# A layer with a top-2 mixture of experts on one core: slot tokens through an inverse table, outputs added to the residual in DRAM

## The chip, the core and the metric

The kernel runs on one core of a Trainium2 chip. Its engines are TensorE (PE), VectorE (DVE), ScalarE (ACT), GpSimd (POOL) and SyncE (SP); each runs its own instruction stream and waits on semaphores. The metric is the device time in microseconds (us) of one execution. Before the change: median 1988.87 us of 3 runs (1988.52 to 1989.82).

## The reference

Input x is 2 x 1024 tokens of 256 floats. First comes a linear-attention layer, then a transformer layer with softmax attention and a mixture of experts, each inside `x + layernorm(layer(layernorm(x)))`. The change is in the experts' part and in what follows it:

```
def moe(h, gate_w, w1, w2, w3):          # E, F, TOPK = 8, 1024, 2
    t = h.reshape(-1, hd)
    probs = softmax(t @ gate_w)
    topw, topi = top_k(probs, TOPK)
    topw = topw / sum(topw)
    combine = zeros((T, E)).at[arange(T)[:, None], topi].add(topw)
    up = einsum('th,ehf->etf', t, w1)
    gated = relu(up) * einsum('th,ehf->etf', t, w3)
    down = einsum('etf,efh->eth', gated, w2)
    return einsum('eth,te->th', down, combine)
h = x + attention(rmsnorm(x, ln1_w), wq, wk, wv, wo)
ffn = h + moe(rmsnorm(h, ln2_w), gate_w, w1, w2, w3)
out = x + layernorm(ffn)                 # x: the input of this block, before its own layernorm
```

## The kernel before

The order of work is written out by hand, one stream for each engine, with semaphores between them. In time it has four stages.

1. Linear attention, up to about 245 us. At its end POOL issues one DMA that writes zeros over all of `xs`, a DRAM buffer of 39 x 128 rows of 1 KB (line 423). While it runs, SP loads the output weights of the second attention, `wo2` (line 326).
2. Softmax attention, 128 tiles, up to about 1432 us. PE is the busiest engine. The residual stream h stands in SBUF as `acc`, 16 tiles of 128 tokens x 256.
3. Router. PE turns h and multiplies it with the gate; DVE works out the two best experts of each token, their shares `topw`, and for each of the 4096 token-expert pairs the row it has in a list sorted by expert, `rowi` (lines 887 to 941). The list is cut into NS = 39 slots of 128 rows; each slot has one expert, `slotei`, and 39 is enough for any routing. Rows of a slot that no token takes are padding. ACT scales h to `t_all` (line 633). Then POOL issues 32 indirect DMAs (line 465), each of which scatters 128 rows of `t_all` to their rows of `xs`. 128 rows of 1 KB are one DMA.
4. Experts, slot by slot. Three chains u = 0, 1, 2 take 13 slots each in turn, so that work item e is slot e // 3 + (e % 3) x 13. SP loads the slot's expert (w1, w3 and w2, 1 MB each, only where the expert changes in the chain), waits for all 32 scatters (line 346) and loads the slot's 128 rows of `xs` (line 347). PE turns them (line 1281), multiplies with w1 and w3 (line 1297), and after relu (ACT, line 652) and product (DVE, line 950) with w2 (line 1306). ACT copies the result to `y_sb` (line 656) and POOL stores it to `ys`, also in DRAM (line 471). When all slots are stored, POOL gathers for each of 16 token tiles two blocks of 128 rows from `ys` (line 477, 32 indirect DMAs), and DVE, a quarter of the tiles at a time, adds them with their weights to `acc` (line 958), takes mean and variance (963, 967), normalises (973), adds to `x_all` (976), and SP stores the tile (line 354).

Every engine stream is in order, so an instruction that waits holds all those behind it.

## Time and profile before

| | us |
|---|---|
| median of 3 runs | 1988.87 |
| the profiled execution, its own time | 1999.07 |
| its span (first to last instruction) | 1997.4 |
| PE busy in the span | 1812.1 (91%) |
| DVE busy | 1061.8 (53%) |
| ACT busy | 910.8 (46%) |
| POOL busy | 234.5 (12%) |
| mean DMA rate over the span | 34 GB/s |

The profile is of one execution, recorded by the hardware profiler; it ran some 10 us longer than the median of the runs without one. Busy shares are means over the four stages. The page's picture of 40 slices of about 50 us shows PE busy at nine tenths or more in nearly all of them, with two places where it isn't: slice 30 (from about 1448 us), where PE is idle and its granted clock is 0.5, and the last one and a half slices, where only DVE and POOL work.

### The profile page before, as it was taken

Reading aid. Unit: us, or ns where it says so; the run is one execution under the profiler, and the core shown is the slowest. Engines: PE = TensorE matmul, PEld = TensorE weight load, DVE = VectorE, ACT = ScalarE, POOL = GpSimd, SP = SyncE. Lnnn points to the kernel's source line nnn. Section 1 sums busy time; section 2 is a strip of 40 time slices with the busy share of each in tenths; the row PEclk is TensorE's granted clock in tenths of the full one; section 3 lists DMA queues with packets and bytes.
Section 4 is the critical chain, followed back from the end, with each engine's and each line's share of the span. In section 5 each row is a group of like instructions: output and inputs, shape, how many; then the busy total and the mean of one; then the engine's idle time right before and its main releaser. Section 6 shows DMA issues by size and latency. Waiting matters only on the chain.

```text
span 1997.4 us, 32462 instructions
## 1 busy us (share of the span) xinstructions
PE 1812.1 (91%) x12222; PEld 1425.7 (71%) x12222; DVE 1061.8 (53%) x2489; ACT 910.8 (46%) x2028; POOL 234.5 (12%) x368
## 2 busy tenths in 40 slices
PE   6999689999999999999999999999907999999970
PEld 5666467777777777777777777777807999999960
DVE  3666566766766766676676676676420111111106
ACT  3433265665666665665565566565511112211210
POOL 2222210000000000000000000000051000000014
PEclk9999899999999999999999999999958999999985
DMA  2000030000000000000000000000034042022413
GB/s 80 0 0 0 28 118 1 9 1 9 1 1 9 1 1 9 1 1 9 1 1 9 1 1 1 1 1 1 1 134 161 24 152 84 26 89 75 161 32 110
DMA packets 44296, 67.22 MB, mean 34 GB/s; under 512 B 9952, under 2 KB 34528, under 8 KB 44192
## 3 DMA queue, kind: packets, MB, share of 16 engines
q1 hardware_dynamic: 35920, 45.11, 6.9%
q0 software_dynamic: 6208, 18.62, 2.8%
q10 hardware_dynamic: 2064, 2.10, 0.3%
q8 instruction: 66, 1.08, 0.2%
q14 instruction: 38, 0.31, 0.1%
HBM read 140.52 MB, written 16.52 MB: 79 GB/s over the span
## 4 chain that ended last, share of the span: by engine, by line
PE 82%; DVE 6%; issue 3%; POOL 3%; ACT 2%; DMA 1%; SPq 1%; another core or an unknown queue 0%; DVEq 0%; POOLq 0%; ACTq 0%
PE wide L1297 14%; PE bank L1219 13%; PE bank L1207 11%; PE bank L1159 8%; PE wide L1191 8%; PE bank L1306 7%; PE wide L1192 7%; PE bank L1228 6%; PE wide L1026 2%; PE bank L1015 2%; POOL xs L465 1%; PE bank L1204 1%; POOL arena L477 1%; ACT qhl L583 1%; PE bank L1083 1%
## 5 line engine op out<-in xcount | busy, mean ns | idle before, releaser
L823 DVE CUSTOM_DVE_ANT_0 arena<-wide,arena 128x896 f32<-128x896 f32 (+7 forms) x512 | 383.6, 754 | 225.1 <-PE wide L1192 221.1
L589 ACT ACTIVATE arena<-arena,nmax 128x896 f32<-128x896 f32 (+7 forms) x512 | 397.1, 776 | 177.4 <-DVE nmax L823 174.3
L1191 PE MATMUL wide<-khi,qhl 128*128 128x512 f32 (+3 forms) x768 | 346.2, 452 | 1.7 <-DVE qhl L816 1.7
L1207 PE MATMUL bank<-ident,arena 128*128 128x128 f32 x2304 | 308.4, 273 | 0.0
L597 ACT COPY arena<-bank 128x512 f32<-128x512 f32 (+1 forms) x352 | 191.7, 545 | 215.4 <-PE bank L1207 206.2
L1297 PEld LDWEIGHTS wide<-wo,arena 128*128 128x128 f32 x2496 | 287.0, 193 | 3.2 <-issue 1.3
L1297 PE MATMUL wide<-wo,arena 128*128 128x128 f32 x2496 | 287.3, 276 | 0.9 <-ACT wo L641 0.9
L1219 PE MATMUL bank<-arena,vt 128*64 128x256 f32 x2304 | 276.9, 385 | 0.0
L950 DVE TENSOR_TENSOR wo<-wide,wo 128x512 f32<-128x512 f32 x78 | 54.0, 692 | 415.3 <-PE wide L1297 415.3
L1207 PEld LDWEIGHTS bank<-ident,arena 128*128 128x128 f32 x2304 | 262.2, 140 | 16.8 <-issue 0.4
L1192 PE MATMUL wide<-klo,qhl 128*128 128x512 f32 (+3 forms) x768 | 256.1, 347 | 0.0
L831 DVE COPY arena<-bank 128x512 f32<-128x512 f32 (+1 forms) x352 | 222.8, 638 | 9.2 <-PE bank L1207 8.5
L1219 PEld LDWEIGHTS bank<-arena,vt 128*64 128x64 f32 x2304 | 154.2, 136 | 91.0 <-issue 20.1
L1191 PEld LDWEIGHTS wide<-khi,qhl 128*128 128x128 f32 x768 | 145.1, 189 | 89.7 <-issue 65.9
L1192 PEld LDWEIGHTS wide<-klo,qhl 128*128 128x128 f32 x768 | 145.8, 190 | 37.1 <-issue 22.5
L1228 PE MATMUL bank<-wo,oT 128*128 128x256 f32 x512 | 135.1, 386 | 12.5 <-DVE oT L848 10.6
L455 POOL COPY arena<-rinv 128x256 f32<-128x256 f32 x128 | 50.9, 398 | 787.2 <-DVE rinv L844 785.2
L1306 PE MATMUL bank<-arena,wo 128*128 128x256 f32 x624 | 141.2, 379 | 0.0
L1306 PEld LDWEIGHTS bank<-arena,wo 128*128 128x128 f32 x624 | 115.5, 190 | 14.1
L652 ACT ACTIVATE wo<-wide 128x512 f32<-128x512 f32 x78 | 46.6, 597 | 173.3 <-PE wide L1297 173.3
L1159 PE MATMUL bank<-rT_all,wq_g 128*128 128x512 f32 x256 | 123.7, 607 | 0.3
L1228 PEld LDWEIGHTS bank<-wo,oT 128*128 128x128 f32 x512 | 87.1, 190 | 25.5 <-DVE oT L848 15.0
(192 smaller groups left out, 1708.4 us busy)
## 6 DMA issues: line engine op xcount, KB each, us to landing
arena<-in_L_ffn_w SPq DMA_DIRECT2D x117, 1024.0 KB
wo<-xs SPq DMA_DIRECT2D x40, 128.0 KB, 2.0
xs<-zeros POOLq DMA_DIRECT2D x1, 4992.0 KB, 20.7
ys<-y_sb POOLq DMA_DIRECT2D x39, 128.0 KB, 2.0
x_all<-in_L_attn_x ACTq DMA_DIRECT2D x1, 2048.0 KB, 9.7
wq_g<-in_L_ffn_wq SPq DMA_DIRECT2D x8, 256.0 KB, 3.3
wo<-in_L_ffn_wo SPq DMA_DIRECT2D x16, 128.0 KB, 8.1
out<-x_all SPq DMA_DIRECT2D x16, 128.0 KB
```

Source lines behind the costliest of these rows:

```text
L589: nc.scalar.activation(probs[t % 2][:, h, 0:w], probs[t % 2][:, h, 0:w], ACT.Exp, bias=nmax[:, t % 2, h:h + 1], scale=-1.0, accum_out=rsum ...
L597: nc.scalar.copy(*turned_to(t, m)).then_inc(S("pT_even"), 1)
L823: nc.vector.tensor_tensor_reduce(out=probs[t % 2][:, h, 0:w], in0=score_bank(t, h)[:, 0:w], in1=causal[:, SEQ - w:SEQ], scale=-1.0, scalar ...
L831: nc.vector.tensor_copy(*turned_to(t, m)).then_inc(S("pT_odd"), 1)
L1159: ins = mm(to, w, rT_all[:, k, at:at + HALF], start=(k == 0), stop=(k == KB - 1))
L1191: mm(dst, q, khi[:, lo:lo + cols], start=True, stop=False)
L1192: ins = mm(dst, q, klo[:, lo:lo + cols], start=False, stop=True)
L1207: ins = nc.tensor.transpose(to[:, h * P:(h + 1) * P], probs[t % 2][:, h, m * P:(m + 1) * P], ident[:])
L1219: ins = mm(bank[2][u * DH:(u + 1) * DH, 0:2 * P], vt[:, n % 2, m], pT[t % 2][m][:, u * 2 * P:(u + 1) * 2 * P], start=(m == 0), stop=(m == ct))
L1228: ins = mm(bank[2][:, 2 * P:2 * P + D], oT[:, j], wo2[:, t // (BATCH * TB), j], start=(j == 0), stop=(j == 1))
L1297: ins = mm(wide[:, at + half, f * P:(f + 1) * P], w[:, k, (half * 4 + f) * P:(half * 4 + f + 1) * P], sT[u][:, k], start=(k == 0), stop=(k ...
L1306: ins = mm(bank[u][:, 0:D], gated[:, f], w2_e[u][:, f], start=(f == 0), stop=(f == FB - 1))
```

## The change

Both scatters of data through DRAM go; three things come in their place.

- The table `rowi` (token to row) is inverted into a table with a column for each slot and a partition for each place in it, which says which token stands there. This is done on PE: with a one-hot matrix of a pair's place in its slot (`inplace`, bf16) as weights and a one-hot matrix of its slot, multiplied with tile number or token number (`worth`, bf16), as the moving side, 32 accumulated matmuls give the token of each row of each slot (`found`, line 1373 of the new kernel), and 32 more the weight of each (`wfound`, line 1377), the float32 weight being split into three bf16 parts. DVE makes the one-hot matrices and reads the results. `fromrow` is the table that is read from (padding reads token 0), `torow` the one that is added to (padding goes to 128 spare rows).
- `t_all` is stored to DRAM (`tbuf`) as it is, in four DMAs of 512 KB. POOL gathers the 128 rows of a slot with one indirect DMA, three slots ahead. `acc` is stored to DRAM too (`hbuf`), in two DMAs of 1 MB.
- ACT scales a slot's output with the weights of its rows as it takes it from PSUM, and POOL adds the 128 rows to their rows of `hbuf` with one indirect DMA that accumulates, each issued only when the one before has landed (semaphore `added`). At the end SP loads `hbuf` back to `acc` in four DMAs, and the final layernorm goes in pairs of tiles: statistics on DVE, normalising on ACT, the last add on POOL. ACT's and POOL's slot loops are written out instead of looping.

The diff, cut to its core:

```
+        tbuf = nc.dram_tensor("tbuf", (NT * P, D), F32, kind="Internal").ap()
+        hbuf = nc.dram_tensor("hbuf", (NT * P + P, D), F32, kind="Internal").ap()
...
 # SP
+            sp.wait_ge(S("acc_done"), BATCH * NKV * TB - TB)
+            sp.dma_start(h_v[:, 0:TB], acc[:, 0:TB]).then_inc(S("h_stored"), 16)
+            sp.wait_ge(S("acc_done"), BATCH * NKV * TB)
+            sp.dma_start(h_v[:, TB:NT], acc[:, TB:NT]).then_inc(S("h_stored"), 16)
+            for i in range(4):
+                tiles = slice(i * (NT // 4), (i + 1) * (NT // 4))
+                sp.wait_ge(S("t_ready"), i + 1)
+                sp.dma_start(t_v[:, tiles], t_all[:, tiles]).then_inc(S("t_stored"), 16)
             sp.wait_ge(S("slots_known"), 1)
...
-                    sp.wait_ge(S("xs_scattered"), 16 * TOPK * NT)
-                    sp.dma_start(xs_sb[u], xs_v[:, bass.ds(slot, 1)].rearrange("p o d -> p (o d)")).then_inc(S(f"xs_loaded{u}"), 16)
...
+            sp.wait_ge(S("added"), 16 * NS)
+            for q in range(4):
+                tiles = slice(q * (NT // 4), (q + 1) * (NT // 4))
+                sp.dma_start(acc[:, tiles], h_v[:, tiles]).then_inc(S(f"h_loaded{q}"), 16)
...
 # POOL
-            gp.dma_start(xs.rearrange("(s p) d -> p s d", p=P), zeros[:]...).then_inc(S("xs_zeroed"), 16)
...
+            def gather(e):
+                u, slot = e % UR, (e // UR + e % UR * RUN) % NS
+                nc.gpsimd.indirect_dma_start(out=xs_sb[u], out_offset=None, in_=tbuf,
+                                             in_offset=bass.IndirectOffsetOnAxis(ap=fromrow[:, slot:slot + 1], axis=0)).then_inc(S(f"xs_loaded{u}"), 16)
+            gp.wait_ge(S("t_stored"), 16 * 4)
+            gp.wait_ge(S("fromrow_ready"), 1)
+            for e in range(UR):
+                gather(e)
+            gp.wait_ge(S("torow_ready"), 1)
+            gp.wait_ge(S("h_stored"), 32)
+            for e in range(NS):
+                u, slot = e % UR, e // UR + e % UR * RUN
+                if e + UR <= NS:
+                    gp.wait_ge(S("sT_psum"), e + 1)
+                    gather(e + UR)
+                gp.wait_ge(S(f"y_ready{u}"), e // UR + 1)
+                if e:
+                    gp.wait_ge(S("added"), 16 * e)
+                nc.gpsimd.indirect_dma_start(out=hbuf, out_offset=bass.IndirectOffsetOnAxis(ap=torow[:, slot:slot + 1], axis=0),
+                                             in_=y_sb[u][:], in_offset=None, compute_op=ALU.add).then_inc(S("added"), 16)
+            for q in range(NT // 2):
+                gp.wait_ge(S("fn_ready"), q + 1)
+                nc.gpsimd.tensor_tensor(x_all[:, 2 * q:2 * q + 2], x_all[:, 2 * q:2 * q + 2], acc[:, 2 * q:2 * q + 2], ALU.add).then_inc(S("out_ready"), 1)
...
 # ACT, at the end of slot e
+                if e == 0:
+                    act.wait_ge(S("weights_known"), 1)
+                if e >= UR:
+                    act.wait_ge(S("added"), 16 * (e - UR + 1))
+                nc.scalar.activation(y_sb[u][:], bank[u][:, 0:D], ACT.Copy, scale=wrow[:, slot:slot + 1]).then_inc(S(f"y_ready{u}"), 1)
...
 # DVE, after rowi: tables
+            step(nc.vector.tensor_tensor(inslot[:], slotnob[:]..., over_slots(slotf[:]), ALU.is_equal))
+            nc.vector.tensor_scalar(worth[:, :, 1], inslot[:], token1[:, 0:1], None, ALU.mult)
+            for kk in range(TOPK):
+                ins = nc.vector.tensor_tensor(worth[:, kk * NT:(kk + 1) * NT, 0], inslot[:, kk * NT:(kk + 1) * NT],
+                                              tileno[:]..., ALU.mult)
+            ins.then_inc(S("worth_ready"), 1)
+            for i in range(4):
+                cs = slice(i * C // 4, (i + 1) * C // 4)
+                nc.vector.tensor_tensor(inplace[:, cs], places[:]..., posf[:, cs]..., ALU.is_equal).then_inc(S("inplace_ready"), 1)
...
+            for i in range(3):
+                ins = nc.vector.tensor_tensor(worth[:, :, 2 + i], inslot[:], over_slots(wsplit[:, i]...), ALU.mult)
+            ins.then_inc(S("worth_ready"), 1)
...
 # PE, ahead of the first slot
+            pe.wait_ge(S("worth_ready"), 1)
+            for c in range(C):
+                pe.wait_ge(S("inplace_ready"), c * 4 // C + 1)
+                ins = mm(bank[2][:, 0:2 * NS], inplace[:, c], worth[:, c, 0:2].rearrange("p v s -> p (v s)"), start=(c == 0), stop=(c == C - 1))
+            ins.then_inc(S("found_psum"), 1)
+            pe.wait_ge(S("worth_ready"), 2)
+            for c in range(C):
+                ins = mm(bank[1][:, 0:3 * NS], inplace[:, c], worth[:, c, 2:5].rearrange("p v s -> p (v s)"), start=(c == 0), stop=(c == C - 1))
+            ins.then_inc(S("wfound_psum"), 1)
```

Between router and first slot, the instructions of PE stand like this (L1281 before and L1385 now turn slot 0, `wo` is a region of SBUF that the slots use for their rows). Before:

```order
L1268 MATMUL wide<-gate,arena 128x8 x32
L1272 MATMUL bank<-picked,tri 128x128
L1273 MATMUL bank<-picked,ones 128x128
L1281 MATMUL bank<-ident,wo 128x128 x2
L1285 UNCONDITIONAL_BRANCH
```

Now:

```order
L1362 MATMUL wide<-gate,arena 128x8 x32
L1366 MATMUL bank<-picked,tri 128x128
L1367 MATMUL bank<-picked,ones 128x128
L1373 MATMUL bank<-worth,inplace 128x78 x32
L1377 MATMUL bank<-worth,inplace 128x117 x32
L1385 MATMUL bank<-ident,wo 128x128 x2
L1389 UNCONDITIONAL_BRANCH
```

Both tables stand ahead of the first slot's turn, the second one too, though only ACT's scaling of the first output needs it. On DVE, from `rowi` (CAST) to the slot loop, where before only the branch into the loop followed:

```order
L1013 TENSOR_SCALAR worth<-inslot,token 128x32x39
L1015 TENSOR_TENSOR worth<-inslot,tileno 128x16x39 x2
L1020 TENSOR_TENSOR inplace<-places,posf 128x1024 x4
L1023 COPY found<-bank 128x78
L1024 SCALAR_TENSOR_TENSOR tok<-found 128x39
L1025 TENSOR_SCALAR fromrow<-tok 128x39
L1036 TENSOR_TENSOR worth<-inslot,wsplit 128x32x39 x3
L1039 COPY wfound<-bank 128x117
```

The second table's input (L1036) comes on DVE only after the first table has been read. On POOL, from the router's power to the end, before:

```order
L397 TENSOR_TENSOR hrstd<-hve,neghalf 128x16
L465 DMA xs<-rT_all,rowi 4992x256 x32
L471 DMA ys<-y_sb 128x256
L477 DMA arena<-ys,rowi 128x256 x32
```

Now (the middle two rows alternate through the 39 slots):

```order
L443 TENSOR_TENSOR hrstd<-hve,neghalf 128x16
L508 DMA wo<-tbuf,fromrow 128x256 x4
L525 DMA hbuf<-y_sb,torow 2176x256
L508 DMA wo<-tbuf,fromrow 128x256
L525 DMA hbuf<-y_sb,torow 2176x256 x3
L529 TENSOR_TENSOR x_all<-x_all,acc 128x512 x8
```

The two runs of 32 indirect DMAs on either side of the slots are gone, and each slot has two of them inside the loop instead of one plain store.

## Rows read from the trace of the kernel before

**Rows 1.** Waits from 1432 us on: who waited for whom, us in total, times, longest

```profile
PE bank L1281 <- DMA wo<-xs: 51.9, 2, 51.1
...
DVE acc L958 <- DMA arena<-ys,rowi: 21.9, 3, 18.5
```

**Rows 2.** Timeline, router to first slot: start us, us, engine, line, operation, [idle before <-releaser]

```profile
1461.60 0.40 SPq L343 DMA_DIRECT2D arena<-in_L_ffn_w  x1
...
1462.01 0.18 DVE L941 CAST rowi<-row 128x32 uint32<-128x32 f32 x1
...
1463.10 1.11 POOL L465 DMA_INDIRECT xs<-rT_all,rowi  x1 [17.20 <-issue]
...
1502.46 0.96 POOL L465 DMA_INDIRECT xs<-rT_all,rowi  x1 [0.30 <-issue]
1505.03 0.34 SPq L347 DMA_DIRECT2D wo<-xs  x1
...
1507.25 0.66 PE L1281 MATMUL bank<-ident,wo 128*128 128x128 f32 x2 [51.05 <-DMA wo<-xs]
...
1508.80 9.63 PE L1297 MATMUL wide<-wo,arena 128*128 128x128 f32 x64 [0.89 <-ACT wo L641]
```

**Rows 3.** Timeline of one slot in the loop

```profile
1533.88 7.31 PE L1297 MATMUL wide<-wo,arena 128*128 128x128 f32 x64
...
1541.24 3.62 PE L1306 MATMUL bank<-arena,wo 128*128 128x256 f32 x16
...
1544.70 7.31 PE L1297 MATMUL wide<-wo,arena 128*128 128x128 f32 x64
1544.90 0.37 ACT L656 COPY y_sb<-bank 128x256 f32<-128x256 f32 x1 [2.83 <-PE bank L1306]
```

**Rows 4.** Windows: us, busy of five engines, granted clock (PEclk), DMA share, GB/s

```profile
1464.00:1468.00 4.00, 0.00 (x0) 0.00 (x0) 0.00 (x0) 0.00 (x0) 3.09 (x4) 0.50 1.00 389
...
1512.00:1516.00 4.00, 4.00 (x31) 4.00 (x31) 0.69 (x1) 0.60 (x1) 0.00 (x0) 0.82 1.02 399
```

**Rows 5.** Operations like the added ones: two groups (busy, mean ns), two timeline rows

```profile
L713 DVE TENSOR_TENSOR arena<-wide,tri 128x1024 f32<-128x1024 f32 x32 | 39.1, 1223 | 11.7 <-PE wide L1026 11.7
...
L411 POOL TENSOR_TENSOR arena<-wo,headmask 128x1024 f32<-128x1024 f32 x16 | 30.0, 1896 | 99.9 <-DVE wo L738 99.9
...
1440.71 6.55 PE L1268 MATMUL wide<-gate,arena 128*128 128x8 f32 x30
...
1448.56 6.47 ACT L633 ACTIVATE rT_all<-acc,hrstd 128x256 f32<-128x256 f32 x16
```

**Rows 6.** Issue to landing of L347, of L471, and of the 2 MB input load

```profile
DMA to landing us min/median/max: 1.9/2.0/13.7
...
DMA to landing us min/median/max: 2.0/2.0/4.8
...
x_all<-in_L_attn_x ACTq DMA_DIRECT2D x1, 2048.0 KB, 9.7
```

**Rows 7.** Timeline from the last slot to the end

```profile
1934.36 0.37 ACT L656 COPY y_sb<-bank 128x256 f32<-128x256 f32 x1 [2.83 <-PE bank L1306]
...
1935.38 0.54 POOL L471 DMA_DIRECT2D ys<-y_sb  x1 [10.28 <-ACT y_sb L656]
1938.25 1.01 POOL L477 DMA_INDIRECT arena<-ys,rowi  x1 [2.33 <-DMA ys<-y_sb]
...
1953.36 1.41 DVE L963 BATCH_NORM_STATS2 stf<-acc 128x6 f32<-128x256 f32 x4
...
1954.80 0.38 DVE L967 BATCH_NORM_AGGREGATE hmean<-stf 128x2 f32<-128x6 f32 x4
...
1955.55 0.18 DVE L970 RECIPROCAL hrstd<-hve 128x4 f32<-128x4 f32 x1 [0.37 <-issue]
...
1993.37 1.42 DVE L976 TENSOR_TENSOR x_all<-x_all,acc 128x256 f32<-128x256 f32 x4
```

**Rows 8.** Timeline at the start of softmax attention

```profile
269.92 1.13 PE L1228 MATMUL bank<-wo,oT 128*128 128x256 f32 x4 [1.92 <-DMA wo<-in_L_ffn_wo]
```

More of the change, by code:

```diff
@@ L458, in _ @@
             power(0, NT, hrstd[:], hve[:], "ve_h", "rstd_h")
-            gp.wait_ge(S("t_ready"), 1)
-            gp.wait_ge(S("rows_known"), 1)
-            gp.wait_ge(S("xs_zeroed"), 16)
-            for t in range(NT):
-                for k in range(TOPK):
-                    nc.gpsimd.indirect_dma_start(out=xs, out_offset=bass.IndirectOffsetOnAxis(ap=rowi[:, k, t:t + 1], axis=0),
-                                                 in_=t_all[:, t], in_offset=None).then_inc(S("xs_scattered"), 16)
@@ L644, in _ @@
             evacuate_slot(0, 1)
-            with act.Fori(0, NS // UR) as it:
-                for u in range(UR):
-                    slot = it * UR + u
-                    for half in range(2):
-                        act.wait_ge(S("up_psum"), slot * 2 + half + 1)
-                        act.wait_ge(S("gated_ready"), slot * 2)
-                        nc.scalar.activation(relu[half], wide[:, half, :], ACT.Relu).then_inc(S("relu_ready"), 1)
-                    evacuate_slot((u + 1) % UR, slot + 2)
-                    act.wait_ge(S(f"slot_done{u}"), it + 1)
-                    act.wait_ge(S(f"ys_stored{u}"), 16 * it)
-                    nc.scalar.copy(y_sb[u][:], bank[u][:, 0:D]).then_inc(S(f"y_ready{u}"), 1)
@@ L659, in _ @@
-            for quarter in range(4):
-                cols = slice(quarter * (NT // 4), (quarter + 1) * (NT // 4))
-                act.wait_ge(S("mean_f"), quarter + 1)
-                nc.scalar.activation(hve[:, cols], hmean[:, cols, 1], ACT.Sqrt, bias=eps[:, 0:1]).then_inc(S("std_f"), 1)
+            for e in range(NS):
+                u, slot = e % UR, e // UR + e % UR * RUN
+                for half in range(2):
+                    act.wait_ge(S("up_psum"), e * 2 + half + 1)
+                    if e:
+                        act.wait_ge(S("gated_ready"), e * 2)
+                    nc.scalar.activation(relu[half], wide[:, half, :], ACT.Relu).then_inc(S("relu_ready"), 1)
+                evacuate_slot((u + 1) % UR, e + 2)
+                act.wait_ge(S(f"slot_done{u}"), e // UR + 1)
+                if e == 0:
[3 more added lines that the diff above has]
+                nc.scalar.activation(y_sb[u][:], bank[u][:, 0:D], ACT.Copy, scale=wrow[:, slot:slot + 1]).then_inc(S(f"y_ready{u}"), 1)
@@ new lines, in _ @@
+            nc.scalar.activation(gsum[:, 0:1], eps[:], ACT.Sqrt).then_inc(S("table_loaded"), 1)
+            act.wait_ge(S("table_loaded"), 3)
+            for q in range(NT // 2 + 1):
+                if q < NT // 2:
+                    cols = slice(2 * q, 2 * q + 2)
+                    act.wait_ge(S("mean_f"), q + 1)
+                    nc.scalar.activation(hve[:, cols], hmean[:, cols, 1], ACT.Sqrt, bias=eps[:, 0:1]).then_inc(S("std_f"), 1)
+                if q:
+                    act.wait_ge(S("nmr_ready"), q)
+                    for i in (2 * q - 2, 2 * q - 1):
+                        ins = nc.scalar.activation(acc[:, i], acc[:, i], ACT.Identity, scale=hrstd[:, i:i + 1], bias=nmr[:, i:i + 1])
+                    ins.then_inc(S("fn_ready"), 1)
@@ L940, in _ @@
             step(nc.vector.tensor_scalar(row[:], row[:], -1.0, None, ALU.add))
-            nc.vector.tensor_copy(rowi[:], row[:]).then_inc(S("rows_known"), 1)
+            step(nc.vector.tensor_copy(rowi[:], row[:]))
+            rows = rowi[:].rearrange("p k t -> p (k t)")
+            nc.vector.tensor_scalar(sloti[:], rows, 7, None, ALU.logical_shift_right)
+            step(nc.vector.tensor_scalar(posi[:], rows, P - 1, None, ALU.bitwise_and))
+            nc.vector.tensor_copy(posf[:], posi[:])
@@ new lines, in _ @@
+            step(nc.vector.scalar_tensor_tensor(out=tok1[:], in0=found[:, 0], scalar=float(P), in1=found[:, 1], op0=ALU.mult, op1=ALU.add))
+            nc.vector.tensor_scalar(fromrow[:], tok1[:], -1.0, 0.0, ALU.add, ALU.max).then_inc(S("fromrow_ready"), 1)
+            step(nc.vector.tensor_scalar(away[:], tok1[:], 0.0, nowhere[:, 0:1], ALU.is_equal, ALU.mult))
+            nc.vector.scalar_tensor_tensor(out=torow[:], in0=tok1[:], scalar=-1.0, in1=away[:], op0=ALU.add, op1=ALU.add).then_inc(S("torow_ready"), 1)
@@ L951, in _ @@
                                                 ALU.mult).then_inc(S("gated_ready"), 1)
[L953 to L956 removed]
+            for q in range(NT // 2 + 1):
+                if q < NT // 2:
+                    tiles = (2 * q, 2 * q + 1)
+                    v.wait_ge(S(f"h_loaded{q // 2}"), 16)
```

156 lines of the change are left out of this document (93 added, 63 removed).

## The prediction

> **What bounds the kernel now.** I read the page's picture of 40 slices first, for where PE is not busy. PE is at nine tenths from the start of attention on but for one slice near 1450 us and the last one and a half. So the question is what stands in those two holes, and whether the part between them stays as it is. Next, the waits from 1432 us on [rows 1]: PE stood 51.1 us for the load of the first slot's rows, and DVE 21.9 us for the gathers at the end. The timelines of the holes then say what fills them.
>
> The front hole [rows 2]: `rowi` is cast at 1462.01, the 32 scatters are issued from 1463.10 to 1502.46, (1502.46 - 1463.10) / 31 = 1.27 us apart, of which each takes POOL 0.96; SP's load of the rows goes out at 1505.03 and PE's first turn is at 1507.25. POOL's issue is the bound there, not the transfer: 128 KB every 1.27 us is 103 GB/s, and the DMA engines gave 389 to 399 GB/s when weights were in flight [rows 4].
>
> The loop [rows 3]: a slot takes 1544.70 - 1533.88 = 10.82 us, of which 7.31 and 3.62 are PE's matmuls. PE does not wait there; ACT, DVE, POOL and SP do. 39 slots therefore end at about 1934.3, where ACT takes the last output [rows 7].
>
> The back hole [rows 7]: from the last output at 1934.3 to the end of the span at 1997.4 it is 63.1 us: store, wait for it, 32 gathers from 1938.25 (at the scatters' pace 41 us), and DVE's chain of the last quarters, whose last add ends at 1994.79; the last store is 2.6 us more.
>
> **The change part by part.** All sums are against the profiled execution, 1999.07 us (span 1997.4). The runs' median is 1988.87, 10.2 lower, and I carry that difference over unchanged.
>
> *The front: PE's first turn.* After the cast ends at 1462.2 DVE has four small table steps (0.1 to 0.2 us each, as the cast's 0.18): 1462.8. For the large ones I take a slope: 1024 elements in 1.22 us [rows 5] is about 0.16 + 1 ns per element, 0.07 less where the next one follows without a wait. The tables are bf16 and no row of before shows a bf16 operation, so this is the value at full length; half of it is the other end, and I take the full length, which the row shows. `inslot` (1248 elements) 1.5, `worth` 1.4 + 2 x 0.75, four `inplace` (1024) 4 x 1.16: together 9.0, so 1471.9 (rounded up for one step's wait). PE follows each quarter as it comes. For one bf16 matmul with new weights: 30 records of the gate's 128x8 float32 take 6.55 us at the low clock, 0.218 each [rows 5]; at the full clock 64 records take 7.31, 0.114 each [rows 3]. PE has been idle, its clock is granted at 0.50 [rows 4], that is 1.2 GHz. bf16 weights are half as wide. Bounds are 0.05 and 0.218; I take 0.15. The last eight are then done at 1473.1, and copy, one combine and the cast to `fromrow` (three steps of 0.2 to 0.25) give 1473.9. POOL starts its DMA 0.9 after the table, as from 1462.19 to 1463.10 [rows 2], issues in 1.1, and the rows land about 1.9 later (rows of L347 and L471 land in 2.0 after issue [rows 6]; a plain load behind weights once took 13.7, a store on POOL's queue at most 4.8). Slot 0 has its rows at 1477.8, at the latest some 1482.
>
> But PE's stream has the second table ahead of the turn (the order of instructions shows it). Its input on DVE comes after `fromrow`: two small steps for `torow`, five for the split (1.1 together with theirs: 1475.2) and three products of 1248 elements, 3 x 1.39 + 0.1 = 4.3: 1479.5. Then 32 matmuls of 0.15, 4.8: 1484.3. The turn is at 1484.3 instead of 1507.25: **23.0 us less**. Bounds: 1478 (bf16 at double rate, then the gather is the later one) and 1487 (0.218 a matmul). The gather is hidden behind the second table by some 6 us.
>
> ACT needs the weights only for the first output, 12 us later. The stores of `t_all` (4 x 512 KB, from 1450 to 1455, at 390 GB/s 1.3 us each) and of `acc` lie under the router's DVE chain, ahead of slot weights on SP's queue, all before `slotei`: nothing. They must not be late for the gather at 1474.8; they have over 15 us.
>
> *Weights of slots 1 and 2.* Before, they were held back behind SP's wait for the scatters and issued after 1505. Now all nine are issued from 1461.6 on. 9 MB at 390 GB/s is 24.2 us: landed by about 1488. Slot 0's three have landed by about 1471, slot 1's by about 1480, wanted at 1497, slot 2's at 1488, wanted at 1508. No wait.
>
> *The clock.* The first slot took 9.63 for work that then takes 7.31, since the clock rose only within 1512 to 1516 [rows 2, 4]. Now PE has some 5 us of table matmuls just ahead of it. Between 0 and 2.3 us less; I take **1.0**.
>
> *The loop.* PE's stream there is the same. POOL has a gather (1.0 to 1.3) and an accumulating scatter (1.0 to 1.3) per slot instead of a store of 0.54, and it now waits for the landing of the add before, with the next add and the gather behind that wait. The gather is three slots ahead, so only a period of POOL over 10.82 counts. A plain scatter lands some 1.5 us after its issue ended (1503.4 to SP's next DMA at 1505.0 [rows 2]). An accumulating one is in no row of before. Lower end: as a plain one, 1.5. Upper end: each of 16 DMA engines has 8 rows, and if it took the whole 2.0 us of a small DMA [rows 6] for each in turn, 16. I take 2.5, near the plain one, one more read of DRAM included. The period would be some 5 us, hidden under PE's 10.82 with 5 to spare: nothing. ACT's scaled copy stands where the plain one was (0.37), its wait for `added` is for the add three slots back.
> The Trainium skill, "Collectives: The Full Stack", on the bandwidth ceiling, says that the DMA engine's inline add costs no cycles of its own but a second source read, so half the rate; by its rule 128 KB would go as 256 KB, at the trace's 390 GB/s 0.3 us more, and the sum would stay. No run of before shows an add.
>
> *The back.* Count from the end of PE's last matmul. Output copied at +0.4, POOL's DMA starts 0.6 later [rows 7], 1.0 issue, 2.5 landing: +4.5. SP issues four loads of 512 KB: the first lands 0.3 + 2.0 + 1.3 later, +8.1, the others 1.3 apart, the last at about +12.1 (2 MB took 9.7 at the start of the kernel, among other loads [rows 6]; that rate would put it at +14.5, still ahead of its use). DVE for a pair: half of 1.41 and of 0.38 [rows 7], 0.90, and two small operations of 0.18, with four waits of 0.04 to 0.05: 1.45. Eight pairs 11.7: +19.8. ACT has 0.3 + 2 x 0.40 per pair (6.47 for 16 [rows 5]) and POOL 1.0 for 512 elements (1.90 for 1024 [rows 5]); both are under 1.45 and only their last ones count: +20.7, +21.8. The last store, 256 KB, 2.6 + 0.4: **+24.8 instead of +63.1, 38.3 less.** Bounds: landing 1.0 less or up to 5 more, POOL up to twice as long per pair (then it is the bound at 2.0 a pair, 5 more).
>
> *Start of attention.* The 5 MB of zeros are gone, and `wo2` was loaded against them: PE stood 1.92 us for it [rows 8]. **2.0 less**, between 0 and 4 (clock). The added constants on POOL (five small ones, under 1 us) lie under the loads of the start.
>
> Sum: 23.0 + 1.0 + 38.3 + 2.0 = 64.3; 1999.07 - 64.3 = 1934.8, and 10.2 off is 1924.6: **1925**. Its own range, from the bounds: 1914 to 1936.
>
> **Rivals.**
>
> A. The adds take the loop (slower). At every slot POOL waits for the landing of the add before. From 9.5 us of landing (10.82 less 1.3 of issue) the loop lengthens by 38 times the excess; from 11.2 us the whole gain is gone (64.3 / 38 = 1.7). At the upper bound of 16 the period is 17.3, and 38 x 6.5 + 13.5 more in the back = 260: 2185. For: the row of a single small DMA is 2.0 us and the rows are read and written back. Against: 32 plain scatters kept a pace of 1.27 us each without falling behind, so rows of an engine are not served one at a time there. 8%.
>
> B. The gain comes, but a part is given back: gathers late behind 9 MB of weights (first turn at 1488 or later, then slots 1 and 2 short of rows), or in the back POOL's adds and DVE's statistics hold each other up (2.5 a pair, 8 more), or loads of `hbuf` at the slow rate of rows 6. For: a load behind weights landed after 13.7 us [rows 6]. Against: that was on the weights' own queue, POOL's queue never took over 4.8. 10 to 20 us less gain: 1935 to 1945. 14%.
>
> C. Faster: bf16 at double rate. DVE's tables take 6 instead of 12 us; then the gather limits, turn at 1478: 1918. For: half the bytes. Against: a broadcast operand in each of them. The Trainium skill, "VectorE: DVE Perf Modes", "What auto-detection actually checks", gives the double rate only where every tensor is 16-bit with step 1 or -1; these have an operand of step 0, so by the page the full length stands and this case falls away. No row of before has a bf16 operation. 8%.
>
> D. It doesn't do what it says: padding. All rows of padding read token 0, up to 128 reads of one row of DRAM, and whole slots of padding come at the end. If reads of one address went one after the other the gather would take longer, but it has 20 us of slack; no change to the sum. It is no case of its own.
>
> **How the numbers follow.** Forecast 70%, A 8%, B 14%, C 8%. A whole loss of the gain needs A. Between 9.5 and 11.2 us of landing A is still faster. Measured differences under 0.2% (4 us) can't be told from none here; 1985 to 1993 needs a landing of about 11: 1%. Slower 8%, faster 91%. Range for 8 in 10: 1912 (C, and the low bounds of the front) to 1942 (most of B).
>
> **What would show it.** In the profile after: PE's first turn near 1482 (after 2 us less at the start), its waiter being the second table and not a DMA; distance of L1401 from slot to slot 10.82; POOL waiting for ACT in the loop and not for `hbuf`; first `hbuf` load some 5 us after the last matmul, and some 25 us from there to the end. It is wrong if POOL's waits in the loop name the DMA to `hbuf`, if PE has idle time in the loop, or if the router's DVE chain past `rowi` takes over 20 us.

## The result, and the profile after

| | before | after |
|---|---|---|
| median of the runs, us | 1989.34 (4 runs, 1988.52 to 1989.85) | 1932.78 (4 runs, 1931.03 to 1934.57) |
| profiled execution / its span, us | 1999.07 / 1997.4 | 1933.22 / 1931.3 |
| ratio of the times | | 0.9716, 95% interval 0.9699 to 0.9733 |

The change takes 56.6 us off the medians. The forecast was 64.3 us less and 1925; the time lies 7.8 us above it and inside its range.

The waits from 1432 us on, as in [rows 1] (who waited for whom: us in total, times, longest):

```profile
POOL hbuf L525 <- ACT y_sb L710: 317.4, 39, 13.2
...
PE bank L1373 <- DVE inplace L1020: 12.6, 4, 11.4
...
DVE stf L1058 <- DMA acc<-hbuf: 11.3, 1, 11.3
...
PE bank L1377 <- DVE worth L1036: 6.4, 1, 6.4
```

PE's 51.1 us for the load of the slot's rows are gone. It waits for DVE's tables instead, 12.6 us in four waits for the first one and 6.4 for the second. POOL waits in the loop for ACT's output and never for the add before, so rival A did not come. DVE's 21.9 us for gathers became 11.3 for one load.

The front, which answers to [rows 2] (timeline: start us, us, engine, line, operation, idle before and its releaser):

```profile
1457.72 0.18 DVE L1002 CAST rowi<-row 128x32 uint32<-128x32 f32 x1
...
1458.54 1.46 DVE L1012 TENSOR_TENSOR inslot<-slotnob,slotf 128x1248 bf16<-128x1248 bf16 x1
...
1460.04 0.55 DVE L1013 TENSOR_SCALAR worth<-inslot,token 128x1248 bf16<-128x1248 bf16 x1
...
1461.93 4.63 DVE L1020 TENSOR_TENSOR inplace<-places,posf 128x1024 bf16<-128x1024 bf16 x4
...
1466.62 0.70 PE L1373 MATMUL bank<-worth,inplace 128*128 128x78 bf16 x8 [0.44 <-DVE inplace L1020]
...
1468.96 1.25 POOL L508 DMA_INDIRECT wo<-tbuf,fromrow  x1 [25.92 <-DVE fromrow L1025]
...
1469.44 4.20 DVE L1036 TENSOR_TENSOR worth<-inslot,wsplit 128x1248 bf16<-128x1248 bf16 x3
...
1473.70 3.33 PE L1377 MATMUL bank<-worth,inplace 128*128 128x117 bf16 x32 [6.38 <-DVE worth L1036]
...
1476.82 0.64 PE L1385 MATMUL bank<-ident,wo 128*128 128x128 f32 x2
...
1478.35 9.60 PE L1401 MATMUL wide<-wo,arena 128*128 128x128 f32 x64 [0.89 <-ACT wo L693]
```

The first turn comes 19.10 us after `rowi`; before, it was 45.24. It stands right behind PE's own second table, with no wait between. The DVE chain and the two table passes on PE are the whole of it.

PE's clock at the first slot (windows as in [rows 4]); the last column is the GB/s of the weights in flight:

```profile
1476.00:1480.00 4.00, 3.11 (x20) 2.72 (x18) 0.68 (x3) 0.62 (x2) 0.95 (x1) 0.50 1.06 398
1480.00:1482.00 2.00, 2.00 (x11) 2.00 (x11) 0.00 (x0) 0.00 (x0) 0.00 (x0) 0.50 1.04 407
1482.00:1484.00 2.00, 2.00 (x16) 2.00 (x16) 0.00 (x0) 0.60 (x1) 0.00 (x0) 0.76 1.03 344
```

It is still granted 0.50 (1.2 GHz) until about 1482, 5 us into the work that follows the turn, although PE had run the tables just before.

One slot in the loop, which answers to [rows 3]:

```profile
1534.73 7.31 PE L1401 MATMUL wide<-wo,arena 128*128 128x128 f32 x64
...
1535.69 1.59 POOL L525 DMA_INDIRECT hbuf<-y_sb,torow  x1 [7.93 <-ACT y_sb L710]
...
1537.58 0.99 POOL L508 DMA_INDIRECT wo<-tbuf,fromrow  x1 [0.30 <-issue]
...
1545.55 4.63 PE L1401 MATMUL wide<-wo,arena 128*128 128x128 f32 x40
```

The distance is 1545.55 - 1534.73 = 10.82 us, unchanged. POOL issues an add in 1.59 and a gather in 0.99, and idles 7.93 before the next. From issue to landing the 39 adds took (min/median/max), and the 40 gathers:

```profile
DMA to landing us min/median/max: 3.7/3.9/7.6
...
DMA to landing us min/median/max: 2.7/2.9/7.2
```

The back, which answers to [rows 7], and below it the closing instructions of two queues (line: duration ns, start us):

```profile
1902.76 0.47 ACT L710 ACTIVATE y_sb<-bank,wrow 128x256 f32<-128x256 f32 x1 [2.83 <-PE bank L1410]
...
1903.51 1.55 POOL L525 DMA_INDIRECT hbuf<-y_sb,torow  x1 [9.25 <-ACT y_sb L710]
...
1907.26 2.02 SPq L387 DMA_DIRECT2D acc<-hbuf  x4
...
1911.18 0.75 DVE L1058 BATCH_NORM_STATS2 stf<-acc 128x6 f32<-128x256 f32 x2 [11.34 <-DMA acc<-hbuf]
...
1914.60 9.95 POOL L529 TENSOR_TENSOR x_all<-x_all,acc 128x512 f32<-128x512 f32 x8 [9.54 <-ACT acc L722]
```

```profile
L87 POOLq DRAIN  x1: 7843/7843/7843, 1923.3 to 1923.3; - x1
...
L87 SPq DRAIN  x1: 13/13/13, 1926.9 to 1926.9; - x1
```

SP had seen its last store land by 1926.9, 24.1 us after the last output. The span ends at 1931.3. What ends last is the closing drain on POOL's queue: it ends at 1923.3 + 7.84 = 1931.1, 6.6 us after POOL's last add (1914.60 + 9.95 = 1924.55).

### The profile page after: what moved, and what is told of

The parts are those of the page before. It is cut to its first block, busy times and chain, and to the rows that moved or that the text cites. A ratio compares the mean times of both kernels' runs of the same rounds, so it can differ in the third digit from the quotient of the medians.

```text
span 1931.3 us, 32217 instructions
## 1 busy us (share of the span) xinstructions
PE 1813.6 (94%) x12286; PEld 1428.7 (74%) x12286; DVE 1055.0 (55%) x2465; ACT 924.1 (48%) x2049; POOL 261.1 (14%) x355
## 4 chain that ended last, share of the span: by engine, by line
PE 86%; DVE 7%; ACT 2%; issue 2%; POOL 1%; DMA 1%; SPq 0%; DVEq 0%; POOLq 0%; ACTq 0%
PE wide L1401 15%; PE bank L1313 13%; PE bank L1301 12%; PE bank L1253 9%; PE wide L1285 8%; PE bank L1410 7%; PE wide L1286 7%; PE bank L1322 6%; PE wide L1120 2%; PE bank L1109 2%; PE bank L1298 1%; ACT qhl L634 1%; PE bank L1177 1%; DVE arena L802 1%; PE bank L1243 1%
## 5 line engine op out<-in xcount | busy, mean ns | idle before, releaser
L1322 PE MATMUL bank<-wo,oT 128*128 128x256 f32 x512 | 135.1, 387 | 11.3 <-DVE oT L909 11.3
L1322 PEld LDWEIGHTS bank<-wo,oT 128*128 128x128 f32 x512 | 87.3, 191 | 24.3 <-DVE oT L909 14.7
```

The source lines that it names most:

```text
L1322: ins = mm(bank[2][:, 2 * P:2 * P + D], oT[:, j], wo2[:, t // (BATCH * TB), j], start=(j == 0), stop=(j == 1))
```

## The experiments

Each batch ran beside the kernel before on the same chip; medians of before were 1989.31, 1990.36 and 1989.69 us.

**e1: the kernel before, unchanged, once more.** Theory: the 10.2 us between its profiled execution and its median are a chance of that execution. No edit.

> The kernel before, unchanged, profiled a second time. The first profiled execution took 1999.07 against a median of 1989, 10 us more; the changed kernel's took 1933.22 against 1932.8. Theory 1: that first execution was a slow one by chance; the profile now is at 1988 to 1991, and the place where the 10 us lay (my guess: the last quarters of the tail, where the trace shows two waits of 3.8 and 2.5 us that it puts down to no engine, and the start) is shorter. Rival: being profiled costs this kernel 10 us, through its 32 gathers or 32 scatters; then it is again at 1997 to 2001. Time ratio 1.000 either way.

Measured: 1989.65 us, ratio 0.9999 (0.9989 to 1.0008), profiled execution 1989.48. So the 10 us were a chance of the one execution. They were not one delay. `rowi` came 3.2 us earlier (1458.79, not 1462.01), the last output 4.2 (1930.20, not 1934.36), and the rest lay behind it: 57.6 us instead of 63.1. DVE's weighing in the back, first of the execution shown before the prediction, then of e1:

```profile
1970.53 1.67 DVE L958 SCALAR_TENSOR_TENSOR acc<-arena,topw,acc 128x256 f32<-128x256 f32 x4 [1.45 <-DMA arena<-ys,rowi]
1976.07 1.67 DVE L958 SCALAR_TENSOR_TENSOR acc<-arena,topw,acc 128x256 f32<-128x256 f32 x4 [3.87 <-remote]
```

```profile
1966.88 3.40 DVE L958 SCALAR_TENSOR_TENSOR acc<-arena,topw,acc 128x256 f32<-128x256 f32 x8 [1.92 <-DMA arena<-ys,rowi]
```

In e1 the third quarter is one piece of eight. In the other it is split, with a wait of 3.87 us that the profile puts down to no engine of this core (`remote`). What caused it stays open.

**e2: zeros later.** The kernel before, with the 5 MB of zeros issued in tile 16 of attention and not ahead of it.

```
-            gp.dma_start(xs..., zeros...).then_inc(S("xs_zeroed"), 16)
...
             for t in range(TILES + 1):
+                if t == 16:
+                    gp.dma_start(xs..., zeros...).then_inc(S("xs_zeroed"), 16)
```

> The kernel before, with its DMA of zeros issued 16 tiles into softmax attention instead of at its start. Theory: the 5 MB stood in the way of the loads of wo2, PE waited 1.9 us for them and then worked some us at half the clock; moved away, PE reaches the end of attention 2.8 us earlier, and the kernel takes 2.5 to 4 us less (ratio 0.998 to 0.999), PE's wait for wo2 being gone. Rival: the 2.8 us come from the removed POOL instruction or the new places in SBUF; then this kernel is within 1 us of before.

Measured: 1989.09 us, ratio 0.9998 (0.9989 to 1.0007): no gain that the medians can show. The zeros had held `wo2` up: its 16 loads land 2.9 us after their issue (median) instead of 8.1, and the last of them is issued at 255.1 and not at 263.7. The wait for `wo2` of [rows 8] is gone. Still the same matmul starts at the same time; its later input is now DVE's `oT`:

```profile
270.00 1.10 PE L1229 MATMUL bank<-wo,oT 128*128 128x256 f32 x4 [0.77 <-DVE oT L849]
```

That the times agree is chance. In the profile before, `oT` came 1.24 us earlier:

```profile
268.19 0.42 DVE L848 TENSOR_TENSOR oT<-bank,arena 128x256 f32<-128x256 f32 x1
```

In e2 it starts at 269.43, because four matmuls of PE ahead of it (line 1160) took 3.54 us and not 1.88: the granted clock was 0.72 between 262 and 268 us in that execution, and 1.00 in both profiles of the kernel before. From the start of `oT` to the start of the matmul it is 0.57 us in e2, 1.73 before and 1.41 in e1. So of the 1.92 us of waiting 1.16 counted, and 0.84 in e1; the rest PE would have waited for `oT`. Attention ended at 1430.32, in e1 at 1430.54.

**e3: the weights' table in slot 0.** The changed kernel, with the 32 matmuls of the second table moved behind the w3 matmuls of slot 0 (`weights_table`), so that the turn needs only the gather.

```
+            def weights_table():
...
+                    if first and u == 0:
+                        weights_table()
                     turn_slot((u + 1) % UR, ...)
```

> The changed kernel, with the 32 matmuls of the second table (the weights) moved from ahead of the first slot's turn to behind slot 0's matmuls with w1 and w3. Theory: in the changed kernel the gather of slot 0, issued at 1469.0, landed 5.9 us later, at 1474.9, under the weights' load; the turn at 1476.8 waited for the second table. So the turn comes 1.9 us earlier at most, and the 32 matmuls cost 1.8 to 3.3 us in the slot: between 1 us faster and 2 us slower than the changed kernel (1931 to 1935). Rival: the forecast's view, in which the gather is hidden by 6 us: then the turn is 4 to 5 us earlier and the kernel 2 to 3 us faster.

Measured: 1936.3 us, ratio 0.9730 (0.9717 to 0.9744), slower than the changed kernel's 0.9716 if anything.

```profile
1474.62 0.66 PE L1386 MATMUL bank<-ident,wo 128*128 128x128 f32 x2 [7.69 <-DMA wo<-tbuf,fromrow]
...
1484.72 1.83 PE L1378 MATMUL bank<-worth,inplace 128*128 128x117 bf16 x32
...
1488.26 3.69 PE L1416 MATMUL bank<-arena,wo 128*128 128x256 f32 x16 [1.47 <-DVE wo L1050]
```

The turn waits for the gather and comes 17.3 us after `rowi`. So the gather had been hidden by only 1.8 us, not by the 6 of the prediction. These went back in slot 0: 1.83 us of matmuls, and 1.47 for DVE, whose first product stood behind its wait for this table. The first output comes 34.65 us after `rowi` (1491.99 - 1457.34), 0.7 later than in the changed kernel. The medians are 3.5 apart, above the 1931 to 1935 expected; what the profile doesn't explain of that stays open.

**e4: three of the eight last adds on DVE.** The changed kernel; POOL is done earlier by three adds.

```
-            for q in range(NT // 2):
+            for q in range(5):
                 gp.wait_ge(S("fn_ready"), q + 1)
...
+            for q in range(5, NT // 2):
+                v.wait_ge(S("fn_ready"), q + 1)
+                nc.vector.tensor_tensor(x_all..., acc..., ALU.add).then_inc(S("out_ready_v"), 1)
```

> The changed kernel, with the last three of POOL's eight adds at the end on DVE, behind its statistics. In the changed kernel the last add ends at 1924.55, the last store has landed at about 1926.7, but the span ends at 1931.3, when POOL's closing drain ends, 6.6 us after its last add. Theory: the drain takes a fixed time from POOL's last work and is what ends the kernel; POOL is now done at about 1920.8, its drain at 1927.4, and the kernel takes 3 to 4 us less than the changed one. Rival: the last stores or the launch's own end set the time; then it is within 1 us of the changed kernel.

Measured: 1929.4 us, ratio 0.9695 (0.9681 to 0.9708), 3.4 less than the changed kernel. The drain moved with POOL's last add, and still ends the span (1927.9):

```profile
1914.89 6.24 POOL L529 TENSOR_TENSOR x_all<-x_all,acc 128x512 f32<-128x512 f32 x5 [9.56 <-ACT acc L722]
```

```profile
L87 POOLq DRAIN  x1: 7850/7850/7850, 1919.8 to 1919.8; - x1
```

It ends at 1927.65, 6.5 us after the last add at 1921.13.

**e5: slots 1 and 2 wait with their weights.** The changed kernel, with one wait on SP.

```
                     sp.wait_ge(S(f"slot_done{u}"), it)
+                    if u == 1:
+                        sp.wait_ge(S("xs_loaded0"), 16)
```

> SP holds back the weights of slots 1 and 2 (6 MB) until gather 0 has landed; nothing else differs from the changed kernel. There gather 0 took 5.9 us from the start of its issue, in a stretch where the DMA engines were full (381 to 409 GB/s), against a median of 2.9 in the slots. Theory (contention): slot 0's 3 MB are done by about 1467, so gather 0 lands 2.9 to 3.5 us after its issue starts, at about rowi + 14.3 instead of rowi + 17.2; the first turn stays at rowi + 19.1, since PE's second table and its 32 matmuls end there, and slots 1 and 2 have their 6 MB by about 1487.5, before slot 1 starts at 1489: time within 1 us of the changed kernel's, 1932.8. Rival (the first gathers are slow in themselves, a queue that was idle): the landing stays near 5.9. Second rival: the held weights are late for slot 1, PE waits there 1 to 4 us and the time is 1934 to 1937.

Measured: 1934.39 us, ratio 0.9715 (0.9701 to 0.9728), that of the changed kernel. Issue to landing of the first four gathers in the changed kernel, then of the first three in e5:

```profile
DMA to landing us min/median/max: 5.9/6.1/6.4
```

```profile
DMA to landing us min/median/max: 2.8/3.0/3.1
```

Between 1470 and 1474 us the DMA engines moved 395 GB/s in the changed kernel; in e5, where these gathers fall between 1471 and 1477, it was 7 to 133. So it was the weights in flight that made the first gathers 3 us slower. The time did not move, because PE's second table ends later than either landing (turn 19.09 us after `rowi`).

**e10: both together.** e5's wait on SP and e3's table in slot 0, and on DVE the result of the table taken behind slot 0's second product (`weights_known`, four lines from L1038 on).

```
+            def weights_known():
...
+                    if first and u == 0:
+                        weights_known()
```

> As e5, and in addition the 32 matmuls of the weights' table run on PE in slot 0 behind the w3 matmuls, with DVE taking their result behind slot 0's second product (in e3 DVE waited for them ahead of the first product, which cost PE 1.47 us and moved the products behind each other). Theory (contention on gather 0, and the table's place): first turn at rowi + 10.2 (fromrow) + 1.1 (issue starts) + 2.9 to 3.5 = rowi + 14.2 to 14.8, against 19.1; the matmuls then cost 1.8 in slot 0 at full clock or up to 3.3 at half, so y of slot 0 comes 1.3 to 3.1 us earlier than in the changed kernel and the time is 1929.7 to 1931.5. Rival (first gathers slow in themselves): turn at rowi + 17, as in e3, and the time is within 1 us of 1932.8. Second rival: an earlier start meets the 6 MB of slots 1 and 2 that now come later, slot 1 waits, and nothing is gained.

Measured: 1929.56 us, ratio 0.9696 (0.9682 to 0.9709), 3.2 less than the changed kernel.

```profile
1471.40 0.66 PE L1395 MATMUL bank<-ident,wo 128*128 128x128 f32 x2 [4.82 <-DMA wo<-tbuf,fromrow]
...
1488.14 0.47 ACT L712 ACTIVATE y_sb<-bank,wrow 128x256 f32<-128x256 f32 x1 [2.83 <-PE bank L1425]
```

The turn is 14.4 us after `rowi` (1456.99), the first output 31.15 after it; in the changed kernel 33.94. The 2.8 between them are this theory's 1.3 to 3.1.

**e8: e10 and four of the last adds on DVE.** As e4, with 4 in place of 5.

> e10's front with the last four of the eight final adds on DVE (e4 had three there, 1929.4). The theory of the tail: POOL's closing drain ends 6.6 us after its last add; with four adds left on POOL that is 1.25 us earlier than in e4, and DVE's own adds end about 1924.4 + store 2.2, so both ends meet at about 24 us behind the last y_sb (28.5 in the changed kernel, 24.9 in e4). Time: 1932.8 - 4.5 (tail) - 1.3 to 3.1 (front, if e10's theory holds) = 1925.2 to 1927.0; 1928.3 if only the tail's holds; 1932 if neither does.

Measured: **1925.92 us**, ratio 0.9676 (0.9663 to 0.9689), below both kernels. Here SP's last store and POOL's drain end nearly together:

```profile
1913.12 4.98 POOL L531 TENSOR_TENSOR x_all<-x_all,acc 128x512 f32<-128x512 f32 x4 [9.29 <-ACT acc L724]
1914.41 8.22 SPq L393 DMA_DIRECT2D out<-x_all  x8
```

SP sees its last store land by 1925.1, and POOL's drain ends at 1916.8 + 7.85 = 1924.65. From the last output (1901.53) to the end of the span (1925.3) it is 23.8 us, expected about 24.

**e12: e8 with a smaller first load of `hbuf`** (pieces of 2, 4, 4 and 6 tiles; `tiles = slice((0, 2, 6, 10)[q], (2, 6, 10, NT)[q])`).

> e8 (1925.9) with the accumulated result loaded in pieces of 2, 4, 4 and 6 tiles in place of four of 4. Theory: the first piece has 256 KB in place of 512 and lands 0.5 to 1.0 us sooner than 3.8, the statistics start so much earlier and every pair behind them too: 1924.9 to 1925.4. Rival (DMA's fixed part dominates, or the later pieces are now late): within 0.3 of 1925.9.

Measured: 1925.16 us, ratio 0.9679 (0.9666 to 0.9693): no difference from e8. The first piece lands 2.7 us after SP's issue instead of 3.8, and the second pair waits for it again:

```profile
1906.72 0.75 DVE L1067 BATCH_NORM_STATS2 stf<-acc 128x6 f32<-128x256 f32 x2 [10.10 <-DMA acc<-hbuf]
...
1908.55 0.75 DVE L1067 BATCH_NORM_STATS2 stf<-acc 128x6 f32<-128x256 f32 x2 [0.80 <-DMA acc<-hbuf]
```

From the last output to the end it is 1923.2 - 1899.54 = 23.7 us, 0.1 less. The median falls into the theory's 1924.9 to 1925.4 by luck: the theory wanted 0.5 to 1.0 us less there.

**e6: three adds per slot.** The changed kernel, with each slot's output added three times, so its output holds three times the experts' part.

```
+                for again in range(3):
+                    if e or again:
+                        gp.wait_ge(S("added"), 16 * (3 * e + again))
                     nc.gpsimd.indirect_dma_start(out=hbuf, ..., compute_op=ALU.add)
```

> Each slot adds its weighed outputs three times into hbuf, one add waiting for the one before (so the result holds three times the experts' part). POOL's chain of a slot is then gather about 1.3 to 1.6 with its wait + 3 adds x (landing 3.9 from issue start + about 0.6 until the next issue starts, 4.5) = 14.8 to 15.5 us, against PE's 10.82. Theory (rival A's cost formula: the loop costs nothing until POOL's chain passes PE's slot, and from there its full length): slots come 14.8 to 15.5 apart, 38 x 4.0 to 4.7 = 152 to 179 us more, and 9 more in the tail: 2094 to 2121. Rival (adds that follow each other overlap or land faster where rows repeat): slots stay at 10.82 and only the tail grows: about 1942. Second rival (landing grows under the weights' traffic, as gather 0's did): over 2130.

Measured: 2033.35 us (one run), 100.6 more than the changed kernel, where 161 to 188 were expected. The threshold is there, its price was too high:

```profile
1603.90 1.55 POOL L526 DMA_INDIRECT hbuf<-y_sb,torow  x1 [2.50 <-DMA hbuf<-y_sb,torow]
1607.86 1.55 POOL L526 DMA_INDIRECT hbuf<-y_sb,torow  x1 [2.41 <-DMA hbuf<-y_sb,torow]
1609.72 1.02 POOL L508 DMA_INDIRECT wo<-tbuf,fromrow  x1 [0.30 <-issue]
1612.34 1.58 POOL L526 DMA_INDIRECT hbuf<-y_sb,torow  x1 [1.60 <-DMA hbuf<-y_sb,torow]
```

An add is 4.0 us behind the one before, and the gather stands inside an add's landing and costs 0.5 more, not 1.3 and its own wait. Over the whole loop the 117 adds start (2006.5 - 1491.5) / 116 = 4.44 us apart, 13.3 per slot; the outputs come (1978.79 - 1490.79) / 38 = 12.84 apart, and the adds still owed stand in the back, 2031.6 - 1978.79 = 52.8 us in place of 28.5. That is 38 x 2.02 + 24.3 = 101.

**e7: two adds per slot** (the same edit with 2; its output holds twice the experts' part).

> Each slot adds its weighed outputs twice (the result holds twice the experts' part). With three adds the slots came 13.3 us apart on the mean, 4.44 for an add with the gather issued inside an add's landing. Theory (a threshold: POOL's chain is free as long as it is under PE's 10.82): two adds are 2 x 4.1 to 4.5 = 8.2 to 9.0 us, under 10.82, so the slots stay at 10.82 and only the tail grows by one add, 3.9 to 4.5: 1936.7 to 1937.3, with the median of the changed kernel at 1932.8. Rival (the added traffic slows weights or gathers, or y_sb buffers come free too late): slots over 11.0 and a time over 1944.

Measured: 1931.79 us, ratio 0.9712 (0.9697 to 0.9727), not the 1937 expected. The loop held: (1901.17 - 1490.07) / 38 = 10.82 a slot. The add of 4.06 more in the back was there too (1901.92 to 1905.98), but the closing drain was shorter:

```profile
1916.99 9.94 POOL L530 TENSOR_TENSOR x_all<-x_all,acc 128x512 f32<-128x512 f32 x8 [9.46 <-ACT acc L723]
```

```profile
L87 POOLq DRAIN  x1: 4088/4088/4088, 1925.6 to 1925.6; - x1
```

It ends 2.8 us after POOL's last add, not 6.6: 28.5 + 4.1 - 3.8 = 28.8, the 1930.0 - 1901.17 measured. The last output itself came 1.6 us earlier than in the changed kernel (1901.17, not 1902.76), because PE's granted clock had risen before the first slot:

```profile
1478.95 7.41 PE L1402 MATMUL wide<-wo,arena 128*128 128x128 f32 x64 [0.89 <-ACT wo L694]
```

That is 7.41 us for the work that took 9.60 in the changed kernel.

**e9: all eight adds on DVE.**

> All eight final adds of the changed kernel on DVE, so POOL's last instruction is the last accumulating DMA, at about last y_sb + 2.3 us. Theory (the closing drain is 6.6 us from POOL's last instruction, whatever it was): it ends near last y_sb + 9 and is hidden; the end is DVE's last add and its store: DVE's statistics end at about +18.5 us, eight adds of 0.7 = 5.6, store 2.2, span ends at +26.5 to 27: time 1930.7 to 1931.3. Rival (the drain starts at the end of all work, or needs POOL's DMA queue to be empty for long, as before's 23.6 us hints): it ends with the kernel, over +28.

Measured: 1930.54 us (one run), from the last output to the end 1928.8 - 1901.99 = 26.8 us, as expected.

```profile
1902.74 1.55 POOL L525 DMA_INDIRECT hbuf<-y_sb,torow  x1 [9.25 <-ACT y_sb L710]
```

```profile
L87 POOLq DRAIN  x1: 8317/8317/8317, 1902.5 to 1902.5; - x1
```

The drain ends at 1910.8, 6.5 us after the issue of the last DMA (1904.29), and is hidden. It hangs on POOL's last instruction, not on the end of the other engines' work.

**e11: the front alone.** The changed kernel's tables and gathers with the old back (`ys`, 32 gathers, weighing on DVE, 16 stores).

```
-                nc.gpsimd.indirect_dma_start(out=hbuf, ..., compute_op=ALU.add).then_inc(S("added"), 16)
+                gp.dma_start(ys_v[:, slot], y_sb[u][:]).then_inc(S(f"ys_stored{u}"), 16)
```

> The changed kernel's front (tables, gathers, weights' table too) with the old back: unweighed outputs stored into their slots' rows, 32 gathers by assignment, DVE's weighing and quarters, eager adds and 16 stores. Theory (the two parts' gains are apart and add up): the router's end to the first turn takes 19.1 us as in the changed kernel against 45.2 before, the tail behind the last y_sb 57.6 us as in the second run of the kernel before, so the time is 1989.4 - 26.1 - about 0.3 = 1963, 30.5 more than the changed kernel. Rival (the front's gain is partly made by the back's edits, for example by the freed POOL queue or ys's rows): tail or slots longer, 1968 or more. Second rival: the tail is 63.1 as in the first profiled execution, because that was a way of the kernel and not a chance: 1968.

Measured: 1962.36 us, ratio 0.9858 (0.9842 to 0.9873); expected 1963.

```profile
1478.64 0.64 PE L1382 MATMUL bank<-ident,wo 128*128 128x128 f32 x2
```

```profile
1904.26 0.38 ACT L707 ACTIVATE y_sb<-bank 128x256 f32<-128x256 f32 x1 [2.83 <-PE bank L1407]
```

The turn is 19.08 us after `rowi` (1459.56), as with both halves, and the back takes 1961.3 - 1904.26 = 57.0, near the 57.6 of e1. So the front works without the new back: it brings 1989.69 - 1962.36 = 27.3 us, and the phases of the table below give 26.1 + 0.3 + 1.0 = 27.4 for it. The back then brings the other 29.6 (1962.36 - 1932.78). A kernel with the new back alone was not built.

## Why the prediction was right, and where it was not

It had the mechanism: both holes shrink, the loop stays, the adds hide. The size is compared with e1, the execution of before that agrees with the median:

| term | predicted, us | measured against e1, us |
|---|---|---|
| front, `rowi` to the first turn | 23.0 | 45.16 - 19.10 = 26.1 |
| clock and loop, first matmul of slot 0 to the last output | 1.0 | 424.70 - 424.41 = 0.3 |
| back, last output to the end of the span | 38.3 | 57.6 - 28.5 = 29.1 |
| start of attention | 2.0 | 1.0 (end of attention 1430.54 - 1429.51) |
| sum | 64.3 | 56.5 |

The sum is 7.8 too high: 9.2 too much for the back, 0.7 for the clock and 1.0 for the start of attention, and 3.1 too little for the front. That the front and the back err in opposite directions is luck.

**The step that failed** is the first sentence on the parts: "The runs' median is 1988.87, 10.2 lower, and I carry that difference over unchanged." The changed kernel's profiled execution is only 0.4 us over its median. The 10.2 were a chance (e1), and 5.5 of them lay in the very hole that the change fills: the prediction took 63.1 us off as the kernel's back and then took the 10.2 off as well. Those 5.5 us were subtracted twice.

**The back.** Its own steps held. Counted from the last output, predicted and measured: add landed +4.5 and +4.5 (SP's load goes out at 1907.26); first statistics +8.1 and +8.4; POOL's last add +21.8 and +21.8; the last store landed +24.8 and +24.1. What was missing is a step behind them, POOL's drain, up to +28.4. In [rows 7] nothing tells of it, since POOL was done long before DVE there. That term was 3.7 too short; e4, e8 and e9 show that it hangs on POOL's last instruction. That POOL's last add came out at +21.8 exactly is in part luck: the pairs followed each other every 1.24 us (eight adds in 9.95) and not every 1.45, and POOL's first add started at +11.8 where the prediction's own steps put it at +10.7 (21.8 - 1.0 - 7 x 1.45).

**The front.** 3 us more than forecast, from small terms. The 32 bf16 matmuls took 3.33 us, 0.104 each, where 0.15 was taken: 1.5. The table of `token1` took 0.55 where 1.4 was taken: 0.85. That one is `TENSOR_SCALAR`; the `TENSOR_TENSOR` tables of the same 1248 elements took 1.46, the full length, so rival C did not come. The Trainium skill, "VectorE: DVE Perf Modes", "The perf-mode tier table", lets a bf16 tensor_scalar go at four times the rate and a tensor_tensor at twice at most. With the rule of step 1 or -1 that the prediction weighed, the rows agree in direction: 0.55 against 1.46 is a factor of 2.7.

"The gather is hidden behind the second table by some 6 us" was wrong by 4 (e3: 1.8): DVE and PE were faster than taken, and the gather took 5.9 us under the weights' load where 1.1 + 1.9 had been taken (e5: 2.8 to 3.1 without that load). This is a small rival B that did happen, and cost nothing while the table stood behind it. e3 paid for it and e10 took it away.

**The clock.** 1.0 was taken, between 0 and 2.3; the first 64 matmuls took 9.60 us, 9.63 before. Table matmuls just ahead brought nothing in that execution. They do not settle it, though: of the seven profiles in which both tables stand ahead of the turn, six have 9.29 to 9.66 us there and one, e7, has 7.41, with a granted clock of 1.00 from 1478 on. The prediction's upper bound occurs too, by chance of the execution; what decides it stays open.

**The start of attention.** The 2.0 is the whole wait of [rows 8], 1.92 us, and that reading was too high: 1.16 of it counted before and 0.84 in e1 (see e2). In all eleven profiled executions with the changed attention the matmul starts 0.57 us after `oT`, as in e2, so about 1 us is gained at that point, and the 1.0 of the table is of that size. Whether it reaches the end of attention is not shown. That end scatters by 1.9 us: 1428.71 to 1430.58 (mean 1429.5) in the eleven, 1432.33 and 1430.54 in two of the kernel before. The latest of the eleven, e5, has the same low clock of 0.72 between 262 and 268 us as e2. And e2's median is only 0.2 us lower, with an interval from 2.2 lower to 1.4 higher.

**Rival A.** The price was bounded by 9.5 us of landing behind the issue. Measured: 3.9 from the start of the issue, 2.3 from its end, near the 2.5 taken. e7 doubles the add and the loop does not move, e6 triples it and the loop lengthens. So the margin was real: with its gather one add takes 4.0 + 0.5 us of POOL's time, two 8.5, three 12.5 and more, against PE's 10.82.

## What to carry to other kernels

If the profiled execution is slower than the median, find out where before sizing a hole: a second profile of the same kernel costs little, and what is late by chance in the hole must not be counted as gain. After an edit that shortens the end of a kernel, ask of every queue when its last instruction is issued, not only of the engine that computes last. And a wait at the head of an engine counts only by its distance to the next input: of the 1.92 us for `wo2` some 1 counted, and the second table hid a gather that came 3 us late. Before calling a wait worthless because nothing moved when it went, compare what led up to it in both profiles: in e2 a low clock ahead of it hid the gain.

## What the runs showed of the hardware beside that

- POOL's closing drain ended 6.5 to 6.6 us after POOL's last instruction, in the changed kernel, e4 and e9 alike, whether that was an add or the issue of a DMA. SP's takes 13 ns. In other kernels it ended at another distance: 2.8 us behind the last add with two adds a slot (e7), 3.8 with three (e6), 8.5 behind the last DMA in e1, where it is 23.6 us long and hidden. The Trainium skill, "VectorE: DVE Perf Modes", "The DRAIN you can't avoid", calls the closing drains constant, about 12 ns on all engines; POOL's here does not agree, and nor do those of PE (2.62 us), ACT (1.12) and DVE (0.98) in the changed kernel, which are over long before the end. What sets POOL's length is open.
- An accumulating DMA of 128 rows of 1 KB into DRAM: 1.55 to 1.64 us of issue, 3.9 from the start of the issue to landing, 4.0 from one add to the next that waits for it.
- An indirect gather of the same size lands in 2.9 us, and in 5.9 to 6.4 when weights come in at some 400 GB/s.
- The same stream on PE met either clock: the first slot's 64 matmuls took 9.60 us in the changed kernel and 7.41 in e7.
- One bf16 matmul of 117 columns with new weights: 3.33 / 32 = 0.104 us at a granted clock of 0.50 and 1.83 / 32 = 0.057 in e3, at the full clock.
